# A decoder kernel on one core: the transposes of the heads' probabilities in a new order on TensorE in two of its attention stages

## The chip, the cores and the metric

The kernel runs on one core of a Trainium2 chip. The metric is the device time of one execution in microseconds (us); lower is better. Each engine of the core (TensorE, VectorE, ScalarE, GpSimd) works through its own list of instructions in order, and SyncE issues the DMAs; they meet only at semaphores. In the rows of the profile TensorE is PE (PEld are its weight loads), VectorE is DVE, ScalarE is ACT, GpSimd is POOL.

## The reference, cut to what matters

Two decoder layers over 16 batches of 256 rows with 512 channels. The two stages that the change touches are the cross attention of the first layer (causal) and the cross attention of the second one, which is followed in the same stage by the last linear layer:

```python
x = x + _L0_attn_ref(_layernorm(x), ...)
x = x + _L0_xattn_ref(_layernorm(x), ctx_1024, ctx_1024, ...)      # stage "cross0"
x = x + _L0_ffn_ref(_layernorm(x), ...)
x = x + _L1_attn_ref(_layernorm(x), ...)
x = x + _L1_xattn_ref(_layernorm(x), ctx_1024, ctx_1024, ...)      # stage "last"
x = x + _L1_ffn_ref(_layernorm(x), ...)                            # stage "last"
...
scores = jnp.einsum('bhqd,bhkd->bhqk', Q, K) / jnp.sqrt(jnp.float32(D_K))
...
attn = jax.nn.softmax(scores, axis=-1)
heads = jnp.einsum('bhqk,bhkd->bhqd', attn, V)
```

There are 16 heads of 32 channels, so a head's scores are 256 by 256, in two tiles of 128 rows (T = 2).

## The kernel before, in words

Five stages run one after the other: self attention, cross attention ("cross0"), the experts, a normed attention, and "last". In cross0 and last each batch of 256 rows is one turn of a loop, and the steps of neighbouring batches are interleaved: a step with "-" belongs to the batch before, one with "+" to the batch after. The order of the steps is written out by hand for each engine in the table ORDERS (from line 175), and each engine executes its own list word by word. `over_batches` (line 94) makes 18 turns of it, of which the first and the last ones hold only the steps whose batch exists.

The steps on TensorE:

- X0, X1: four transposes each of the normed rows; Q0 to Q3: projections for four heads each (24 matmuls in cross0, where the keys are made too, 12 in last); V: values (cross0 only); O0, O1: output projection of a half of the rows, 12 matmuls of 512 columns.
- S0 to S3: scores of four heads into four PSUM banks, one bank for each head of a group.
- T0 to T15: the transposes of one head's probabilities (three in cross0, four in last), `prob_transposes`, lines 659 and 2124. All heads use the same single PSUM bank, TP. So T of head h waits until the copy of head h-1 out of the bank is done (`wait_taken`), and until GpSimd has normalised head h (`norm_ok`).
- PV0 to PV3: probabilities times values for four heads, `times_v`, lines 673 and 2137: eight matmuls, for the first 128 keys the four heads, then for the last 128 keys the four heads. Only the latter count up `pv_ok`.
- F0, F1, G0, G1: the last linear layer (last only).

The steps on the other engines: "take h" is the copy of TP into one of eight buffers `probT` (odd heads on ScalarE, even ones on VectorE). It waits for T of its head, and, as the buffer is used again every eight heads, for PV of head h-8:

```python
def take(n, h, off):
    dve.wait_ge(t_full, n * H + h + 1)
    after(dve, pv_ok, n, H, h - NPT + 1, off)
    dve.tensor_copy(probT[:, h % NPT, :], TP[:, :]).then_inc(pt_dve, 1)
```

"z v" takes the result of PV v out of the bank Z, first on ScalarE (after PV v, `heads_hi`), then on VectorE (`heads_lo`), after which PV v+1 may start. "max h" (VectorE), "exp h" (ScalarE), "inv h" (VectorE) and "norm h" (GpSimd) make the softmax of head h from its scores; "mask" stands before "max" in cross0. On ScalarE the order around the changed place of cross0 is `take13- z2- take15- Q2 exp4`.

Of the kernel before, what the change touches and what calls it, by code (L numbers as in the profile page):

```python
# [132 lines left out]
class Uses:  # L133
# [20 lines left out]
    def adds(self, key, n):  # L154
# [4 lines left out]
        while True:  # L159
# [3 lines left out]
            if r > self.n_batch or batch_of(r, self.keys[i][1], self.n_batch) is not None:  # L163
# [27 lines left out]
    },  # L191
    "cross0": {
        "PE": (
                "S0 PV1- T12- Q2 T13- Q3 T14- S1 PV2- T15- T0 PV3- T1 V00 T2 S2 T3 V01 T4 O0- T5 S3 T6 X0+ X1+ T7 PV0 T8 O1- T9 "
                "Q0+ T10 Q1+ T11"),
        "ACT": (
                "take13- z2- take15- Q2 exp4 z3- exp5 take1 Q3 exp6 exp7 take3 exp8 exp9 C0+ exp10 exp11 take5 C1+ X0+ take7 "
# [8 lines left out]
    },  # L206
    "last": {
        "PE": (
                "Q2 T15- S1 PV3- T0 Q3 T1 O0- X0+ T2 S2 X1+ T3 O1- T4 Q0+ T5 S3 T6 Q1+ T7 PV0 T8 T9 PV1 T10 F0- F1- S0+ T11 G0- "
                "T12 G1- T13 PV2 T14"),  # L210
        "ACT": (
                "take13- exp2 z2- exp3 take15- z3- Q2 exp4 exp5 exp6 Q3 take1 exp7 X0+ X1+ take3 exp8 exp9 exp10 exp11 Q0+ "
                "take5 exp12 Q1+ take7 exp13 z0 exp14 take9 exp15 F0- F1- take11 exp0+ z1 exp1+"),
        "DVE": (
# [3 lines left out]
        "POOL": (  # L218
                "rstd+ norm2 norm3 norm4 norm5 norm6 norm7 norm8 norm9 frstd- res norm10 norm11 norm12 norm13 norm14 fbias- "
# [2262 lines left out]
```

## Time and profile before

| | us |
|---|---|
| median of 3 runs | 3359.61 (3356.51 to 3359.7) |
| the profiled execution, its own time | 3358.55 |
| its span, first to last instruction | 3356.8 |
| PE busy | 3053.1 |
| DVE busy | 2104.7 |
| ACT busy | 1418.3 |
| POOL busy | 1315.6 |

The span is 1.75 us shorter than the same execution's own time. A row of the timeline gives start and duration; a matmul is pipelined, so the next step can start before the end that is shown for the one before.

### The profile page before, as it was taken

Reading aid. Unit: us, or ns where it says so; the run is one execution under the profiler, and the core shown is the slowest. Engines: PE = TensorE matmul, PEld = TensorE weight load, DVE = VectorE, ACT = ScalarE, POOL = GpSimd, SP = SyncE. Lnnn points to the kernel's source line nnn. Section 1 sums busy time; section 2 is a strip of 40 time slices with the busy share of each in tenths; the row PEclk is TensorE's granted clock in tenths of the full one; section 3 lists DMA queues with packets and bytes.
Section 4 is the critical chain, followed back from the end, with each engine's and each line's share of the span. In section 5 each row is a group of like instructions: output and inputs, shape, how many; then the busy total and the mean of one; then the engine's idle time right before and its main releaser. Section 6 shows DMA issues by size and latency. Waiting matters only on the chain. (4 is left out here: it accounts for less than half of the span.)

```text
span 3356.8 us, 72149 instructions
## 1 busy us (share of the span) xinstructions
PE 3053.1 (91%) x23800; PEld 2292.0 (68%) x23800; DVE 2104.7 (63%) x5290; ACT 1418.3 (42%) x4627; POOL 1315.6 (39%) x1983
## 2 busy tenths in 40 slices
PE   7999999999998799999988888878879996999997
PEld 6788888888887688778854433333357774777775
DVE  7676666667664888888862222122157776888885
ACT  5344444444443555555551111111122224777774
POOL 3454454455443344444420000000012224888886
PEclk9999999999998999999999999999889997999999
DMA  3000000100000211111269999999831113222221
GB/s 123 32 19 25 31 19 19 37 19 19 25 25 26 89 61 64 50 50 56 79 247 424 431 433 431 431 431 432 371 122 59 58 56 112 75 86 73 87 84 35
DMA packets 108792, 448.74 MB, mean 134 GB/s; under 512 B 11636, under 2 KB 30072, under 8 KB 100280
## 3 DMA queue, kind: packets, MB, share of 16 engines
q1 hardware_dynamic: 102520, 429.56, 32.7%
q10 hardware_dynamic: 6208, 18.35, 1.4%
q8 instruction: 36, 0.59, 0.1%
q14 instruction: 28, 0.23, 0.0%
HBM read 395.45 MB, written 52.43 MB: 133 GB/s over the span
## 5 line engine op out<-in xcount | busy, mean ns | idle before, releaser
L513 POOL TENSOR_TENSOR cross_prob<-cross_prob,cross_rsum 128x128 f32<-128x128 f32 (+1 forms) x512 | 255.3, 528 | 345.7 <-DVE cross_rsum L960 345.4
L513 POOL TENSOR_TENSOR self_prob<-self_prob,self_rsum 128x128 f32<-128x128 f32 (+1 forms) x512 | 287.2, 587 | 245.0 <-DVE self_rsum L960 244.9
L1988 POOL TENSOR_TENSOR last_prob<-last_prob,last_rsum 128x256 f32<-128x256 f32 x512 | 298.3, 612 | 91.9 <-DVE last_rsum L2324 89.6
L766 ACT ACTIVATE self_prob<-self_S,self_neg_max 128x128 f32<-128x128 f32 (+1 forms) x512 | 211.9, 425 | 207.3 <-DVE self_neg_max L952 207.1
L1621 POOL MEMSET norm_minus_half<- 128x2 f32 x1 | 0.1, 99 | 716.6 <-POOLq L52 716.6
L507 POOL TENSOR_TENSOR self_QK_T<-self_QK_T,self_turned 128x512 f32<-128x512 f32 x128 | 166.3, 1299 | 281.1 <-DVE self_QK_T L876 279.3
L2203 ACT ACTIVATE last_prob<-last_S,last_neg_max 128x256 f32<-128x256 f32 x512 | 238.4, 492 | 20.7 <-DVE last_neg_max L2320 20.6
L766 ACT ACTIVATE cross_prob<-cross_S,cross_neg_max 128x128 f32<-128x128 f32 (+1 forms) x512 | 210.2, 429 | 76.8 <-DVE cross_neg_max L952 75.8
L1505 DVE COPY experts_hidT<-experts_T 128x512 f32<-128x512 f32 x32 | 22.1, 692 | 285.0 <-PE experts_T L1394 285.0
L2320 DVE TENSOR_REDUCE last_neg_max<-last_S 128x2 f32<-128x512 f32 x256 | 166.1, 682 | 31.4 <-PE last_S L2114 30.3
L2134 PE MATMUL last_T<-last_ident,last_prob 128*128 128x128 f32 x1024 | 161.8, 281 | 19.1 <-DVE last_probT L2329 15.3
L974 DVE SCALAR_TENSOR_TENSOR self_zTl<-self_Z,self_bv_c,self_zTh 128x256 fp32r<-128x256 f32 x128 | 61.3, 479 | 181.3 <-ACT self_zTh L787 181.3
L2134 PEld LDWEIGHTS last_T<-last_ident,last_prob 128*128 128x128 f32 x1024 | 112.8, 141 | 75.6 <-issue 44.7
L952 DVE TENSOR_REDUCE self_neg_max<-self_S 128x1 f32<-128x128 f32 (+1 forms) x512 | 153.8, 347 | 4.8 <-issue 4.2
L81 PE MATMUL self_A<-self_xTh,self_wqh 128*128 128x256 f32 x512 | 150.8, 294 | 5.2 <-DVE self_xTl L861 5.2
L952 DVE TENSOR_REDUCE cross_neg_max<-cross_S 128x1 f32<-128x128 f32 (+1 forms) x512 | 153.2, 349 | 1.1
L787 ACT ACTIVATE self_zTh<-self_Z,self_bv_c 128x256 fp32r<-128x256 f32 x128 | 60.9, 475 | 211.1 <-PE self_Z L687 211.1
L81 PE MATMUL self_A<-self_xTh,self_wkh 128*128 128x256 f32 x512 | 149.1, 291 | 0.0
L670 PE MATMUL cross_T<-front_ident,cross_prob 128*128 128x128 f32 x768 | 132.8, 282 | 17.7 <-ACT cross_probT L775 11.2
L670 PE MATMUL self_T<-front_ident,self_prob 128*128 128x128 f32 x768 | 131.4, 280 | 18.2 <-POOL self_prob L513 9.3
L83 PE MATMUL self_A<-self_xTh,self_wkl 128*128 128x256 f32 x512 | 145.2, 284 | 0.0
L83 PE MATMUL self_A<-self_xTh,self_wql 128*128 128x256 f32 x512 | 145.0, 283 | 0.0
(332 smaller groups left out, 9713.7 us busy)
## 6 DMA issues: line engine op xcount, KB each, us to landing
late_x<-in_L_ffn_w SPq DMA_DIRECT2D x32, 4096.0 KB, 38.8
moe_w<-in_L_ffn_w SPq DMA_DIRECT2D x31, 4096.0 KB, 38.5
front_spare<-in_ctx SPq DMA_DIRECT2D x32, 512.0 KB, 8.3
front_x_t<-in_x SPq DMA_DIRECT2D x16, 512.0 KB, 3.6
self_res<-in_x SPq DMA_DIRECT2D x16, 512.0 KB, 3.6
x<-self_res SPq DMA_DIRECT2D x16, 512.0 KB, 2.8
front_x_t<-x SPq DMA_DIRECT2D x16, 512.0 KB, 5.4
cross_res<-x SPq DMA_DIRECT2D x16, 512.0 KB, 3.6
```

The costliest lines, as they stand in the source:

```text
L81: pe.matmul(out, ah, bh, start=first, stop=False)
L83: mm = pe.matmul(out, al, bh, start=False, stop=last)
L507: pool.tensor_tensor(to, to, turned.rearrange("p a s -> p (a s)"), ALU.add).then_inc(rot_ok, 1)
L513: ins = pool.tensor_tensor(pr, pr, rsum[:, h, t:t + 1].to_broadcast([P, KQ[t]]), ALU.mult)
L670: mm = pe.transpose(TP[:, o:o + P], prob[:, h % NP, SOFF[t] + k * P:SOFF[t] + (k + 1) * P], ident[:, :])
L766: ins = act.activation(prob[:, h % NP, SOFF[t]:SOFF[t] + KQ[t]], SC[h % G][:, SOFF[t]:SOFF[t] + KQ[t]], ACT.Exp, bias=neg_max[:, h, t:t + ...
L952: ins = dve.tensor_reduce(neg_max[:, h, t:t + 1], SC[h % G][:, SOFF[t]:SOFF[t] + KQ[t]], AX.X, ALU.max, negate=True)
L974: dve.scalar_tensor_tensor(zTs[1][:, v, :], Z[:, 0:S], bv_c[:, v:v + 1], zTs[0][:, v, :], ALU.add, ALU.subtract).then_inc(z_ok, 1)
L1988: ins = pool.tensor_tensor(pr, pr, rsum[:, h, t:t + 1].to_broadcast([P, S]), ALU.mult)
L2134: mm = pe.transpose(TP[:, o:o + P], prob[:, h % NP, t * S + k * P:t * S + (k + 1) * P], ident[:, :])
L2203: ins = act.activation(prob[:, h % NP, t * S:(t + 1) * S], SC[h % G][:, t * S:(t + 1) * S], ACT.Exp, bias=neg_max[:, h, t:t + 1], scale=1. ...
L2320: dve.tensor_reduce(neg_max[:, h, :], SC[h % G][:, :].rearrange("p (t k) -> p t k", t=T), AX.X, ALU.max, negate=True).then_inc(max_ok, 1)
```

## The change

Only words in the orders move. In cross0, on TensorE, T15 of the batch before goes from behind PV2 to ahead of it. In last, T3 to T8 on TensorE each move ahead of the step that stood before them, so that in a full turn no two T are neighbours. The copies take3, take5 and take7 on ScalarE and take4 and take6 on VectorE each move ahead of one step too; take8 stays in its place.

```diff
     "cross0": {
         "PE": (
-                "S0 PV1- T12- Q2 T13- Q3 T14- S1 PV2- T15- T0 PV3- T1 V00 T2 S2 T3 V01 T4 O0- T5 S3 T6 X0+ X1+ T7 PV0 T8 O1- T9 "
+                "S0 PV1- T12- Q2 T13- Q3 T14- S1 T15- PV2- T0 PV3- T1 V00 T2 S2 T3 V01 T4 O0- T5 S3 T6 X0+ X1+ T7 PV0 T8 O1- T9 "
                 "Q0+ T10 Q1+ T11"),
...
     "last": {
         "PE": (
-                "Q2 T15- S1 PV3- T0 Q3 T1 O0- X0+ T2 S2 X1+ T3 O1- T4 Q0+ T5 S3 T6 Q1+ T7 PV0 T8 T9 PV1 T10 F0- F1- S0+ T11 G0- "
+                "Q2 T15- S1 PV3- T0 Q3 T1 O0- X0+ T2 S2 T3 X1+ T4 O1- T5 Q0+ T6 S3 T7 Q1+ T8 PV0 T9 PV1 T10 F0- F1- S0+ T11 G0- "
                 "T12 G1- T13 PV2 T14"),
         "ACT": (
-                "take13- exp2 z2- exp3 take15- z3- Q2 exp4 exp5 exp6 Q3 take1 exp7 X0+ X1+ take3 exp8 exp9 exp10 exp11 Q0+ "
-                "take5 exp12 Q1+ take7 exp13 z0 exp14 take9 exp15 F0- F1- take11 exp0+ z1 exp1+"),
+                "take13- exp2 z2- exp3 take15- z3- Q2 exp4 exp5 exp6 Q3 take1 exp7 X0+ take3 X1+ exp8 exp9 exp10 exp11 "
+                "take5 Q0+ exp12 take7 Q1+ exp13 z0 exp14 take9 exp15 F0- F1- take11 exp0+ z1 exp1+"),
         "DVE": (
...
-                "inv6 X1+ max10 inv7 max11 inv8 inv9 O1- take4 fstats- inv10 max12 take6 max13 max14 inv11 max15 take8 z0 fapply- "
+                "inv6 X1+ max10 inv7 max11 inv8 inv9 take4 O1- fstats- inv10 take6 max12 max13 max14 inv11 max15 take8 z0 fapply- "
                 "inv12 inv13 inv14 take10 max0+ max1+ max2+ take12 z1 inv15 inv0+ G0- G1-"),
```

## Rows read from the trace of the kernel before

**Rows 1.** The page, busy time, share of the span and instructions of each engine.
```profile
PE 3053.1 (91%) x23800; PEld 2292.0 (68%) x23800; DVE 2104.7 (63%) x5290; ACT 1418.3 (42%) x4627; POOL 1315.6 (39%) x1983
```
**Rows 2.** Windows inside cross0, the experts and last: busy time, PEclk the granted clock.
```profile
1150.00:1690.00 540.00, 528.76 (x4718) 431.66 (x4718) 459.71 (x1461) 314.62 (x1209) 238.36 (x475) 1.00 0.18 64
1780.00:2420.00 640.00, 525.90 (x3532) 259.17 (x3534) 132.36 (x248) 75.16 (x92) 0.00 (x0) 0.93 1.01 431
2850.00:3300.00 450.00, 437.58 (x4029) 329.39 (x4030) 377.99 (x961) 344.04 (x1176) 381.88 (x584) 1.00 0.25 79
```
**Rows 3.** TensorE's waits in the window of cross0: total us, times, longest.
```profile
PE cross_T L670 <- ACT cross_probT L775: 9.9, 15, 0.7
```
**Rows 4.** TensorE's waits in the window of last.
```profile
PE last_T L2134 <- DVE last_probT L2329: 11.0, 14, 0.8
```
**Rows 5.** Timeline of TensorE in cross0: PV2-, T15-, T0, PV3- (start, duration).
```profile
1417.84 0.86 PE L687 MATMUL cross_Z<-cross_probT,cross_V 128*32 128x256 f32 x16
1418.63 0.55 PE L670 MATMUL cross_T<-front_ident,cross_prob 128*128 128x128 f32 x3
1419.83 0.55 PE L670 MATMUL cross_T<-front_ident,cross_prob 128*128 128x128 f32 x3 [0.66 <-ACT cross_probT L775]
1420.31 0.86 PE L687 MATMUL cross_Z<-cross_probT,cross_V 128*32 128x256 f32 x16
```
**Rows 6.** Timeline of ScalarE at the same place: z2-, take15-.
```profile
1418.84 0.38 ACT L785 ACTIVATE cross_zTh<-cross_Z 128x256 fp32r<-128x256 f32 x1 [3.26 <-PE cross_Z L687]
1419.29 0.49 ACT L775 ACTIVATE cross_probT<-cross_T 128x384 f32<-128x384 f32 x1
```
**Rows 7.** Timeline of VectorE at the same place: take14-.
```profile
1417.17 0.56 DVE L967 COPY cross_probT<-cross_T 128x384 f32<-128x384 f32 x1 [1.01 <-PE cross_T L670]
```
**Rows 8.** Timeline of TensorE in last: S2, X1+, T3, first of O1-.
```profile
3081.15 1.15 PE L2114 MATMUL last_S<-last_KT,last_QT 32*128 32x256 f32 x16
3082.23 0.66 PE L2063 MATMUL last_A<-last_ident,last_x_t 128*128 128x128 f32 x4
3082.72 0.60 PE L2134 MATMUL last_T<-last_ident,last_prob 128*128 128x128 f32 x4
3083.07 0.48 PE L81 MATMUL last_A<-last_woh,last_zTh 128*128 128x512 f32 x1
```
**Rows 9.** The same turn: S3, T6, first of Q1+; T7, PV0, T8, T9.
```profile
3088.32 1.15 PE L2114 MATMUL last_S<-last_KT,last_QT 32*128 32x256 f32 x16
3089.39 0.66 PE L2134 MATMUL last_T<-last_ident,last_prob 128*128 128x128 f32 x4
3089.81 0.36 PE L81 MATMUL last_A<-last_xTh,last_wqh 128*128 128x256 f32 x1
...
3091.32 0.60 PE L2134 MATMUL last_T<-last_ident,last_prob 128*128 128x128 f32 x4
3091.84 1.07 PE L2149 MATMUL last_Z<-last_probT,last_V 128*32 128x256 f32 x16
3092.85 0.66 PE L2134 MATMUL last_T<-last_ident,last_prob 128*128 128x128 f32 x4
3094.29 0.66 PE L2134 MATMUL last_T<-last_ident,last_prob 128*128 128x128 f32 x4 [0.78 <-DVE last_probT L2329]
```
**Rows 10.** Timeline of ScalarE in that turn: take3; exp12's two passes, take7.
```profile
3083.41 0.59 ACT L2210 ACTIVATE last_probT<-last_T 128x512 f32<-128x512 f32 x1
...
3090.21 0.47 ACT L2203 ACTIVATE last_prob<-last_S,last_neg_max 128x256 f32<-128x256 f32 x1 [1.18 <-DVE last_neg_max L2320]
...
3090.67 0.47 ACT L2203 ACTIVATE last_prob<-last_S,last_neg_max 128x256 f32<-128x256 f32 x1
...
3091.97 0.59 ACT L2210 ACTIVATE last_probT<-last_T 128x512 f32<-128x512 f32 x1
```
**Rows 11.** Timeline of VectorE in that turn: take8.
```profile
3093.54 0.69 DVE L2329 COPY last_probT<-last_T 128x512 f32<-128x512 f32 x1 [0.82 <-PE last_T L2134]
```
**Rows 12.** Timeline of GpSimd in that turn: norm6 to norm9.
```profile
3084.04 4.73 POOL L1988 TENSOR_TENSOR last_prob<-last_prob,last_rsum 128x256 f32<-128x256 f32 x8
```

## The prediction

> **What bounds the kernel now.** I read the page first: PE is busy for 91% of the span and no other engine for more than 63% [rows 1]. That is a mean over five stages, so I took windows inside the two stages that the change touches. In cross0 TensorE is busy for 528.8 of 540 us, in last for 437.6 of 450, both at a granted clock of 1.00 [rows 2]. TensorE sets the pace of both, and it stands still for only 11 and 12 us of these windows. Next I read TensorE's waits there, to see whether that little is one thing. It is: in cross0 one wait of 0.66 us in each of 15 turns, 9.9 us in all, before T0, ended by a copy on ScalarE [rows 3, 5]; in last one of 0.78 us in each of 14 turns, 11.0 us, before T9, ended by take8 on VectorE [rows 4, 9]. Last I read the timeline of one turn around each place, on every engine, because the question for a reordering is always the same: for each T, when does the copy of the head before it end, and what does that copy wait for.
>
> What the reader should see is that a copy needs three things: its own T, its turn in its engine's list, and a free `probT` buffer, which is to say PV of the head eight before. The order on TensorE covers a copy only if the covering step is not itself what the copy waits for.
>
> All other waits of TensorE in a turn come later than these, and are on copies and evictions that TensorE itself sets off. So what one turn loses at either place moves everything behind it, and I count it in full.
>
> **The change, cross0.** T15 moves ahead of PV2. It can start where PV2 starts now, at 1417.84: take14 ends at 1417.73 [rows 5, 7]. PV2 then starts 0.48 later, the distance from a T to the PV behind it (1419.83 to 1420.31) [rows 5].
> Now the chain that releases T0. On ScalarE the list is z2-, take15-. z2 starts 1.00 after PV2 starts, take15 0.45 after z2, and T0 0.54 after take15 (1417.84, 1418.84, 1419.29, 1419.83) [rows 5, 6]. So T0 comes 1.99 after PV2's start whatever T15 does, since take15 stands behind z2 and z2 waits for the end of PV2. T15 is today inside that time: it ends at 1419.18 and costs nothing. Moved ahead, it costs its 0.48, and PV2 covers nothing of its copy: T0 at 1417.84 + 0.48 + 1.99 = 1420.31 in place of 1419.83.
> That is 0.48 x 15 = 7.2 us. In the turn that drains the stage, S1 and T0 have no batch. T14 and T15 are neighbours there, so T15 can't start earlier than now (it waits for take14), and PV3 comes 0.48 + 1.99 = 2.47 after T15's start instead of T15's 0.55, the 0.11 to its copy (1419.18 to 1419.29), 0.49 and 0.05 = 1.20: 1.3 us more. Cross0: 8.5 us slower.
>
> **The change, last, up to S3.** No step is added; what counts is where the copies get no cover. Distances from start to start: S to the next step 1.08, X1 to T 0.49, T to O1 0.35 [rows 8]; S to T 1.07, T to Q 0.42, the Q block to T 1.51, T to PV0 0.52, PV0 to T 1.01 [rows 9].
> Today S2 to the first matmul of O1 is 3083.07 - 3081.15 = 1.92, with X1 and T3 between. Afterwards it is T3, X1, T4. T4 waits for take3, and only X1 stands between: T3 takes 0.66 behind an S (T6 does), its copy starts 0.03 later (T8 ends 3093.51, take8 starts 3093.54), lasts 0.59, and T4 follows 0.06 behind it (3094.23 to 3094.29) [rows 9 to 11]: 1.34. Without a wait it would be about 0.49 + 0.49 = 0.98 (T to X is not in the trace; I take X to T, four transposes each, bounds 0.35 and 0.52). O1 then starts 1.08 + 1.34 + 0.35 = 2.77 after S2: 0.85 later than today, of which 0.36 is a new stall and the rest the T that is now ahead of S3 instead of behind it. T5, T6 and T7 have O1 (twelve matmuls of 512 columns), Q0 (1.51 us) and S3 (1.07) before them, more than the 0.03 + 0.69 + 0.06 that a copy needs beyond its T's end. So S3 is 0.85 later.
>
> **From S3 to T9.** Today that is 3094.29 - 3088.32 = 5.97 [rows 9]. Afterwards the order is S3, T7, Q1, T8, PV0, T9. T8 waits for take7, and on ScalarE take7 now stands close behind S3 with exp12 ahead of it. exp12 needs the scores of S3 and their maximum, and starts 1.89 after S3's start (3090.21); its two passes take 0.46 each (3090.21, 3090.67), so take7 starts 2.81 and ends 3.40 after S3, and T8 starts at 3.46 where its place in the list would allow 1.07 + 0.42 + 1.51 = 3.00: a second new stall, 0.46. Today exp12 hides under Q1.
> PV0 follows at 3.98. Then take8: it needs the buffer of head 0, so it waits for PV0 itself. PV0's counts come from its last four matmuls, which run side by side, so it is as good as the end of PV0: 1.07, and 0.14 to the start of the waiting instruction (PV2's end 1418.70, z2 1418.84 [rows 5, 6]). take8 starts at 5.19, ends at 5.88, T9 at 5.94. PV0 covers nothing of take8; the distance PV0 to T9 is 1.96 where 1.01 would do.
> So S3 to T9 is 0.03 shorter, and the turn is 0.85 - 0.03 = 0.82 us longer. Counted by stalls: 0.36 + 0.46 + 0.95 = 1.77 come, and the one stall that goes is worth 1.44 - 0.49 = 0.95 (T8 to T9, less what one T needs behind another). Behind T9 the order is as before, and z0, the last linear layer's input and F0 follow take8 as today, later by the same time.
> GpSimd isn't in the way: norm6 to norm9 are done at 3084.04 + 4.73 = 3088.77, norm8 a quarter of that stretch earlier, while T8 would run after 3091 [rows 12]. The DMAs of SyncE hang on S, PV and X1 in an unchanged order, and their data is needed a turn later. 16 turns have these steps; the first and last ones lack some neighbours, and I count them as full ones with 1.5 us either way: 0.82 x 16 = 13.1 us.
>
> **Sum.** 8.5 + 13.1 = 21.6. From the profiled execution's own 3358.55 that is 3380.2; the median of the runs shown is 1.1 higher, so I predict 3381.
>
> A row and a rule of the Trainium skill on the clock: it is 1.00 in both windows though each turn has its stall [rows 2]. The page "TensorE: Matmul & The Clock Gate", section "Part 4: PE-mode transpose", says that transposes don't count as a busy PE in the same way, which would speak against stalls placed among transposes. That is the rival on the clock below, and the trace so far speaks against it.
>
> **Rivals.**
> - *The copies do get cover* (faster). If take15 were ready with T15 and take8 with T8, both stalls would go: 0.66 x 15 + 0.95 x 16 = 25 us, 3334. It turns on one point, whether a copy waits for the PV that now stands behind its T. For T15 it does through z2 in ScalarE's list, for T8 through `pv_ok`; were PV0's count for head 0 early in PV0, some of it would come. Against it: the four counts come together at its end. The Trainium skill, "Perfetto Trace Analysis", section "Matmuls", asks that independent groups use other PSUM banks so that the eviction of one overlaps the next; PV0 writes another bank than T8 and by that rule alone the change would gain as this rival says. 3 in 100.
> - *Only cross0 pays.* In last the waits for take3 and take7 may be shorter than my chain (0.36 and 0.46 would have to vanish), and last comes out even: + 8.5, 3368. 6 in 100.
> - *Absorbed.* A wait later in each turn that doesn't hang on the moved steps takes the delay up, and the time stays at 3360. The waits of TensorE show no second one per turn [rows 3, 4]. 4 in 100.
> - *The clock falls.* More stalls in a turn could bring the granted clock of both stages to what the experts' stage has, 0.93 [rows 2]: (528.8 + 437.6) x 0.075 = 73 us on top, 3454; a part of it is likelier than all. 3 in 100.
> - The forecast: 84 in 100.
>
> **Range.** For the forecast alone: cross0 7.2 to 10; last 0.5 to 1.15 a turn, from the bounds of T to X, from a T4 that hardly waits to copies that each start 0.1 later than I take, so 8 to 18.5. That gives 3375 to 3389. With the rivals nearest to it I give 3371 to 3391. A change of 0.2% (6.7 us) is about what a measurement of this kernel can tell from none. Faster 0.03, within 0.04, slower 0.93.
>
> **What would show it.** In cross0 of the changed kernel: PV2 0.48 behind T15, and T0 still 1.99 behind PV2, with about 1.1 us of idle time before it; the turn 0.48 longer. In last: a T3-T4 distance of 1.34, T8 3.46 and T9 5.94 behind S3, and three waits a turn where one was. The clock 1.00 in both. The prediction is wrong if T0 follows PV2 by less than 1.9, if take8 starts before PV0's end, or if take7 goes ahead of exp12's second pass.

## The result, and the profile after

The median of four runs is 3385.5 us (3381.9 to 3388.3) against 3359.1 (3356.5 to 3359.7): a ratio of 1.0079, with a 95% interval from 1.0065 to 1.0093, or 26.4 us more. (The kernel before now has four runs; the three known before the prediction gave 3359.6.) The profiled execution took 3387.97, 2.5 above the median; its span is 3386.2.

The same rows as before, read in the same order. The page: TensorE is busy for 7 us more than in [rows 1], in a span that is 29 us longer, so most of the loss is waiting, not work.

```profile
PE 3060.1 (90%) x23800; PEld 2295.0 (68%) x23800; DVE 2107.7 (62%) x5290; ACT 1414.3 (42%) x4627; POOL 1314.7 (39%) x1983
```

The same windows of cross0 and last as in [rows 2], then TensorE's waits in each (the first row stands for cross0, beside [rows 3]; the other three for last, beside [rows 4]). Columns of the windows: stretch, length, busy time of PE, PEld, DVE, ACT and POOL, granted clock, DMA share, GB/s.

```profile
1150.00:1690.00 540.00, 524.34 (x4673) 427.58 (x4672) 457.12 (x1446) 308.85 (x1194) 236.44 (x472) 1.00 0.18 63
2850.00:3300.00 450.00, 425.81 (x3888) 318.46 (x3889) 368.76 (x930) 330.79 (x1136) 365.79 (x563) 1.00 0.25 78
```

```profile
PE cross_T L670 <- ACT cross_probT L775: 14.6, 15, 1.1
...
PE last_T L2134 <- DVE last_probT L2329: 11.7, 14, 0.9
PE last_T L2134 <- ACT last_probT L2210: 10.2, 27, 0.8
PE last_A L2095 <- DVE last_xb L2309: 1.2, 8, 0.2
```

In cross0 the one wait of each turn is longer, 0.97 in place of 0.66. In last the wait on VectorE's copy is still there, and 27 waits on ScalarE's copies, two a turn, have come beside it. The clock stays at 1.00.

TensorE around the changed place of cross0 (start, duration): T15, PV2, T0, PV3. It answers to [rows 5].

```profile
1418.11 0.55 PE L670 MATMUL cross_T<-front_ident,cross_prob 128*128 128x128 f32 x3
1418.59 0.86 PE L687 MATMUL cross_Z<-cross_probT,cross_V 128*32 128x256 f32 x16
1420.41 0.55 PE L670 MATMUL cross_T<-front_ident,cross_prob 128*128 128x128 f32 x3 [0.96 <-ACT cross_probT L775]
1420.88 0.86 PE L687 MATMUL cross_Z<-cross_probT,cross_V 128*32 128x256 f32 x16
```

ScalarE there: z2-, then take15-, as in [rows 6].

```profile
1419.59 0.38 ACT L785 ACTIVATE cross_zTh<-cross_Z 128x256 fp32r<-128x256 f32 x1 [3.74 <-PE cross_Z L687]
1419.87 0.48 ACT L775 ACTIVATE cross_probT<-cross_T 128x384 f32<-128x384 f32 x1
```

T15 has long been done when ScalarE comes to its copy: ScalarE first waits for PV2, takes z2 out, and only then turns to T15. PV2 covers nothing.

TensorE in a full turn of last: S2, T3, X1, T4, the first matmul of O1; then S3, T7, T8, PV0, T9. It answers to [rows 8] and [rows 9].

```profile
3097.91 1.15 PE L2114 MATMUL last_S<-last_KT,last_QT 32*128 32x256 f32 x16
3098.98 0.65 PE L2134 MATMUL last_T<-last_ident,last_prob 128*128 128x128 f32 x4
3099.47 0.60 PE L2063 MATMUL last_A<-last_ident,last_x_t 128*128 128x128 f32 x4
3100.41 0.63 PE L2134 MATMUL last_T<-last_ident,last_prob 128*128 128x128 f32 x4 [0.34 <-ACT last_probT L2210]
3100.80 0.48 PE L81 MATMUL last_A<-last_woh,last_zTh 128*128 128x512 f32 x1
...
3106.05 1.15 PE L2114 MATMUL last_S<-last_KT,last_QT 32*128 32x256 f32 x16
3107.13 0.66 PE L2134 MATMUL last_T<-last_ident,last_prob 128*128 128x128 f32 x4
...
3109.60 0.63 PE L2134 MATMUL last_T<-last_ident,last_prob 128*128 128x128 f32 x4 [0.38 <-ACT last_probT L2210]
3110.15 1.07 PE L2149 MATMUL last_Z<-last_probT,last_V 128*32 128x256 f32 x16
3112.06 0.66 PE L2134 MATMUL last_T<-last_ident,last_prob 128*128 128x128 f32 x4 [0.83 <-DVE last_probT L2329]
```

ScalarE in that turn: take3; the first pass of exp12, take7. It answers to [rows 10].

```profile
3099.67 0.60 ACT L2210 ACTIVATE last_probT<-last_T 128x512 f32<-128x512 f32 x1 [1.50 <-PE last_T L2134]
...
3107.94 0.47 ACT L2203 ACTIVATE last_prob<-last_S,last_neg_max 128x256 f32<-128x256 f32 x1 [1.66 <-DVE last_neg_max L2320]
...
3108.86 0.60 ACT L2210 ACTIVATE last_probT<-last_T 128x512 f32<-128x512 f32 x1
```

VectorE in that turn: take8, which answers to [rows 11].

```profile
3111.31 0.69 DVE L2329 COPY last_probT<-last_T 128x512 f32<-128x512 f32 x1 [1.55 <-PE last_Z L2149]
```

The reader should look at the releaser in that row. In [rows 11] it was `last_T`, the transpose; now it is `last_Z`, which is PV0. T8 started 1.7 us before, and its copy still can't start, since it writes into the buffer of head 0 that PV0 reads.

From first to last matmul of the stage, cross0 takes 627.7 us in place of 619.6 (+8.1), last 574.0 in place of 549.9 (+24.1). From the start of one PV3 to the next (PV3 closes a batch; the medians over the full turns), a turn of cross0 takes 37.96 in place of 37.62, and one of last 33.27 in place of 32.18. The two stages together lose 32.2 and the span 29.4, because the stages that the change leaves alone took 2.8 less in this execution than in the one before.

The two ends of last cost more than their share in these two executions. Of its 24.1, 14 turns carry 14 x 1.08 = 15.1; the way to the first PV3 carries 3.9, the last interval 3.5, and the stretch behind it 1.6. TensorE in the first turn: T4, then T5.

```profile
2831.79 0.63 PE L2134 MATMUL last_T<-last_ident,last_prob 128*128 128x128 f32 x4 [0.34 <-POOL last_prob L1988]
2834.99 1.09 PE L2134 MATMUL last_T<-last_ident,last_prob 128*128 128x128 f32 x4 [2.57 <-DVE last_probT L2329]
```

VectorE there: the low half of X1, max10, max11, inv8 and inv9, then take4.

```profile
2832.17 0.69 DVE L2277 TENSOR_TENSOR last_xTl<-last_A,last_xTh 128x512 fp32r<-128x512 f32 x1 [0.39 <-ACT last_xTh L2191]
2832.78 0.68 DVE L2320 TENSOR_REDUCE last_neg_max<-last_S 128x2 f32<-128x512 f32 x1
...
2833.45 0.67 DVE L2320 TENSOR_REDUCE last_neg_max<-last_S 128x2 f32<-128x512 f32 x1
2834.03 0.22 DVE L2324 RECIPROCAL last_rsum<-last_sums 128x2 f32<-128x2 f32 x2
2834.17 0.67 DVE L2329 COPY last_probT<-last_T 128x512 f32<-128x512 f32 x1
```

The first turn has no O1 that could stand between T4 and T5. T4 starts at 2831.79, but take4 stands behind inv9 in VectorE's list. VectorE waits 0.39 for ScalarE's half of X1 and from there works without a pause through everything up to take4. In the order before, the Q0 block stood between T4 and T5. Here TensorE waits 2.57 us, and then T5 takes 1.09 in place of some 0.63. Windows of the first turn, of the last interval of last and of the last matmuls of cross0 show why T5 is slow:

```profile
2834.00:2841.00 7.00, 6.01 (x36) 5.35 (x36) 1.70 (x6) 2.85 (x10) 6.68 (x10) 0.52 0.06 23
3342.00:3349.00 7.00, 6.09 (x47) 3.13 (x45) 2.99 (x13) 3.37 (x13) 4.53 (x9) 0.54 0.01 4
1717.20:1720.30 3.10, 3.08 (x8) 2.47 (x9) 2.81 (x6) 0.00 (x0) 3.10 (x1) 0.59 0.34 131
```

The granted clock is 0.52 to 0.59 here, near the lower of its two levels. Whether the change brings that about is a question for the experiments.

### The profile page after: what moved, and what is told of

It is laid out like the page before. It is cut to its first block and busy times, and to the rows that moved or that the text cites. A ratio compares the mean times of both kernels' runs of the same rounds, so it can differ in the third digit from the quotient of the medians.

```text
span 3386.2 us, 72149 instructions
## 1 busy us (share of the span) xinstructions
PE 3060.1 (90%) x23800; PEld 2295.0 (68%) x23800; DVE 2107.7 (62%) x5290; ACT 1414.3 (42%) x4627; POOL 1314.7 (39%) x1983
## 3 DMA queue, kind: packets, MB, share of 16 engines
q1 hardware_dynamic: 102520, 429.56, 32.6%
## 5 line engine op out<-in xcount | busy, mean ns | idle before, releaser
L82 PE MATMUL self_A<-self_xTl,self_wqh 128*128 128x256 f32 x512 | 145.1, 283 | 0.0
```

The source lines that it names most:

```text
L82: pe.matmul(out, ah, bl, start=False, stop=False)
```

## The experiments

Those of each group ran on one chip, with runs of the kernel before among them: median 3358.7 for the first four, 3359.4 for the last three. "Before" and "after" below are the two kernels of the change. Turns are from one S2 or PV3 to the next, and stage times are those of the profiled execution, which in several kernels is not the median one.

**Cross0 alone.** Only the word in cross0 moves, last is as before.

```diff
-  S1 PV2- T15- T0        (TensorE, cross0)
+  S1 T15- PV2- T0
```

> The order of cross0 as changed, that of last as before. My theory (T0 hangs on PV2, then z2, then take15; T15 ahead of PV2 pushes that chain back): T15 to PV2 0.48, PV2 to T0 1.82, no less; each full turn 0.36 longer, the stage 8 us longer, the time 3367. Rival (the stages act on each other through the clock or the data, and cross0 alone is harmless): 3360.

Measured: 3364.0 (3359.7 to 3368.7), ratio 1.0017 [1.0008, 1.0026], so 5.3 us. Cross0 takes 627.7, as in the whole change, with turns of 37.93 and T0 1.82 behind PV2. The turns and T0 are as expected; the time is 3 us short of the expected 3367, while the profiled execution took 3366.9. In that execution last takes 2.6 more than before though its order and its turns are unchanged: its last matmuls ran in a stretch with a granted clock of 0.53.

```profile
3336.00:3343.00 7.00, 5.83 (x21) 4.09 (x14) 0.48 (x1) 0.47 (x1) 0.06 (x1) 0.53 0.21 77
```

So up to 2.6 us at the end of last may come whatever order it has, and are not to be put down to the change. The reverse holds for cross0: in the profile of the run with take7 ahead of exp12 (below), where cross0 has its old order, the first 3.4 us of its last twenty-four matmuls ran at a clock of 0.51 and the stretch behind PV3 took the same 1.6 longer.

**Last alone.** Last as changed, cross0 as before.

> The order of last as changed, that of cross0 as before. My theory: three waits a turn (0.34 before T4, 0.38 before T8, 0.83 before T9), a turn 1.1 longer, plus 9 us in the first turn and the drain, where the clock falls to half: the stage 24 us longer, the time 3380 to 3384. If the steady turns were all of it, 3375. The two single changes add up to the whole (26 us) within 4 us if the stages don't act on each other.

Measured: 3377.2 (3376.1 to 3382.8), 1.0060 [1.0047, 1.0074], so 18.6 us; last takes 574.0 with turns of 33.27, the same as in the whole change. That is between the two expectations, 3375 for the full turns alone and 3380 to 3384 with 9 us at the ends; the profiled execution, 3382.8, is the slowest of the five, so its 24 us for last is more than the usual cost. The parts add up, 5.3 + 18.6 = 23.9 against 26.4, within what these medians can tell: nothing shows that the two edits act on each other.

**Sixteen buffers.** It takes away what take8 waits for. Last as changed, but each head has a `probT` of its own.

```diff
-    NP = NPT = 8
+    NP, NPT = 8, 16
...
-                after(dve, pv_ok, n, H, h - NPT + 1, off)
+                after(dve, pv_ok, n, H, 1 if off < 0 else h - NPT + 1, off)
```

> As e2, but last has 16 buffers for the transposed probabilities in place of 8, so that take8 no longer waits for PV0. My theory (take8 waits for PV0 through the buffer): the wait of 0.83 before T9 goes, T9 follows PV0 by 1.0 instead of 1.9, a turn is 0.8 shorter than in e2, 12 us in all, and the other two waits stay. Rival (take8 is late because VectorE's list is full with the maxima, or since T8 itself is late): T9 stays 1.9 behind PV0 and the time stays that of e2.

Measured: 3380.5 (3374.6 to 3382.7), 1.0063 [1.0048, 1.0078]; last 573.6, turns 33.41. No gain; the expectation of some 12 us was missed. TensorE and VectorE show where it went. TensorE: PV0, T9, the first matmuls of PV1.

```profile
3072.01 1.07 PE L2149 MATMUL last_Z<-last_probT,last_V 128*32 128x256 f32 x16
3073.01 0.66 PE L2134 MATMUL last_T<-last_ident,last_prob 128*128 128x128 f32 x4
3074.36 0.42 PE L2149 MATMUL last_Z<-last_probT,last_V 128*32 128x256 f32 x4 [0.69 <-DVE last_zTl L2333]
```

VectorE: take8, z0.

```profile
3072.21 0.69 DVE L2329 COPY last_probT<-last_T 128x512 f32<-128x512 f32 x1 [0.58 <-PE last_T L2134]
3073.82 0.48 DVE L2333 SCALAR_TENSOR_TENSOR last_zTl<-last_Z,last_bv_c,last_zTh 128x256 fp32r<-128x256 f32 x1 [0.92 <-ACT last_zTh L2216]
```

The mechanism is confirmed: with its own buffer take8 runs beside PV0, and T9 follows PV0 by 1.00, without a wait. But PV1 needs the bank Z that PV0 has filled, and now waits for z0; it starts 2.35 behind PV0, where in the kernel after it was 2.49. Of the 0.83 that went, 0.69 came back at once, one step further on. The turn is even 0.14 longer: T4 waits 0.42 in place of 0.34 and F0 some 0.30 for VectorE where it had waited 0.15 or not at all. I had priced the wait before T9 and not looked at what is late next. This kernel also bears on the clock: it has the same wait before T5 in the first turn, 2.56, yet ran the 9 us behind it, and the last interval too, at a clock of 1.00.

```profile
2830.80:2840.00 9.20, 8.12 (x84) 6.40 (x88) 4.68 (x12) 6.02 (x22) 7.16 (x11) 1.00 0.08 25
3338.00:3351.00 13.00, 9.96 (x96) 5.73 (x96) 7.12 (x21) 7.14 (x21) 11.24 (x17) 1.00 0.01 2
```

**take7 ahead of exp12.** It takes away the wait before T8. Last as changed, one pair exchanged on ScalarE.

```diff
-  take5 Q0+ exp12 take7 Q1+        (ScalarE, last)
+  take5 Q0+ take7 exp12 Q1+
```

> As e2, but on ScalarE take7 stands ahead of exp12. My theory (T8 waits for take7, and take7 for exp12, exp12 for the maximum of S3): the wait of 0.38 before T8 goes, T8 follows S3 by 3.0 to 3.1 instead of 3.55, a turn is 0.4 to 0.5 shorter than in e2, 6 us in all. Rival (the maximum on VectorE or GpSimd's pass is what T8 waits for, not the order on ScalarE): no change from e2, or longer, as exp12 to exp15 come later and S0 of the next batch waits for them.

Measured: 3369.5 (3364.4 to 3371.6), 1.0031 [1.0019, 1.0042]. The turn is 32.66, 0.61 shorter than with last as changed. TensorE's waits in last:

```profile
PE last_T L2134 <- DVE last_probT L2329: 11.7, 14, 0.8
PE last_T L2134 <- ACT last_probT L2210: 4.8, 14, 0.3
```

The 14 waits on ScalarE before T8 are gone (27 became 14), those before T4 and T9 are as they were. So the wait before T8 is caused by exp12 standing ahead of take7, as the prediction says, and it is worth what it shows (0.38) and somewhat more. In the profiled executions last is 14.1 shorter than with last alone: 14 x 0.61 = 8.5, and the rest lies at the ends, whose drain (44.1 against 48.4 from the last S2 on) ran here at a clock of 1.00 up to the wait for the last F0. The medians differ by 7.7, close to the turns' share alone (6 was expected).

**The copy of T15 ahead of z2.** Cross0 as changed, last as before.

```diff
-  take13- z2- take15-        (ScalarE, cross0)
+  take13- take15- z2-
```

> cross0 as changed, and on ScalarE take15 ahead of z2; last as before. My theory (T0 hangs on z2 only through the order on ScalarE): T0 follows PV2 by 0.8 instead of 1.82 and its wait of 0.96 goes. But PV3 waits for z2 on both engines, and from PV2's start that chain is 1.0 + 0.42 + 0.42 and a few hundredths, so PV3 can't come earlier than 1.9 to 2.0 behind PV2 and takes over a wait of about 0.6; a turn comes out 0.1 shorter than before to 0.1 longer, the time 3358 to 3360. If nothing else waited, the turn would be 0.7 shorter than before and the time 3349. Rival (T0 waits for something else, take14 or GpSimd's pass): no change from the changed cross0 alone, 3364.

Measured: 3367.6 (3359.7 to 3370.6), 1.0023 [1.0013, 1.0032]; turns of 37.83. TensorE: PV2, T0, PV3, then T1.

```profile
1419.82 0.86 PE L687 MATMUL cross_Z<-cross_probT,cross_V 128*32 128x256 f32 x16
1420.61 0.55 PE L670 MATMUL cross_T<-front_ident,cross_prob 128*128 128x128 f32 x3
1421.72 0.86 PE L687 MATMUL cross_Z<-cross_probT,cross_V 128*32 128x256 f32 x16 [0.56 <-DVE cross_zTl L972]
1422.83 0.44 PE L670 MATMUL cross_T<-front_ident,cross_prob 128*128 128x128 f32 x2 [0.26 <-DVE cross_probT L967]
```

T0 now starts 0.79 behind PV2 and waits for nothing: it was z2 in ScalarE's list that held it. But PV3 waits for z2 0.56, and T1 0.26 for take0, which VectorE comes to late because its own half of z2 is late. Two waits replace one, 0.82 for 0.97. The turn is 0.13 shorter than with cross0 as changed and still 0.21 longer than before, and the time, 8.2 above the kernel before, shows no gain: the expected 3358 to 3360 was missed. The wait of PV3 had been foreseen, that of T1 had not. It is the buffers' result again: PV3 now follows PV2 by 1.90, which is PV2 and both halves of z2, and no order of the T's would make that shorter (this last is argued, not tried).

**The old order at the ends.** Last as changed, but its first and its last turn have the order of before on TensorE, ScalarE and VectorE.

```diff
+    def steps_of(e, full, r):
+        return EDGE[e] if isinstance(r, int) and r in (0, n_batch - 1) else full
```

> As e2, but the first full turn of last and the turn of the last batch run in the order of before on TensorE, VectorE and ScalarE; all turns between are as changed. My theory (of the 24 us in this stage 9 come from these two turns, with the clock at half in them): the stage 559 + 14 turns of 1.08 = 565 us in place of 574, the clock 1.00 where it was at half in the first turn, the time 3370. Rival (the loss belongs to the full turns, the clock would fall anyway): no change from e2.

Measured: 3372.0 (3371.5 to 3373.7), 1.0045 [1.0030, 1.0061]. Last takes 564.7 with unchanged turns of 33.27, both as expected; the other 9.3 us of last alone's 574.0 were at its ends. By the medians the ends are worth less, 3377.2 - 3372.0 = 5.2. A window of the first turn, of last alone, then of this kernel:

```profile
2826.00:2838.00 12.00, 9.03 (x70) 7.34 (x64) 7.15 (x19) 7.01 (x25) 9.52 (x16) 0.86 0.21 67
```

```profile
2826.00:2838.00 12.00, 10.09 (x100) 7.44 (x100) 6.95 (x20) 10.06 (x38) 10.88 (x18) 1.00 0.21 68
```

The clock is at 1.00 here again, and so it is in the last interval. But that alone doesn't show that the old order keeps it there. Three other kernels with the wait of 2.56 or 2.57 before T5 (sixteen buffers, take7 ahead of exp12, and the last kernel below) were also at 1.00 in the 8 to 9 us behind it, and the drain of the old order ran partly at the lower level in the profiles of cross0 alone and of the copy of T15. So the ends' loss has two parts. With no fall right behind T5 the way to the first PV3 takes 51.9 with take7 ahead of exp12 and 48.9 here, and at a clock of 1.00 the last interval takes 31.2 with sixteen buffers and 30.2 here: about 4 us belong to the order. The other 5 or so are the clock's. This split is an estimate, since it borrows from kernels that differ in one thing more and the first of them has a short fall further on.

**Both copies put right.** The change, with take15 ahead of z2, take7 ahead of exp12 and Q1 on ScalarE behind exp14, and on TensorE PV0 ahead of T8, so that Q1 covers PV0's end and take8.

```diff
-  T7 Q1+ T8 PV0 T9                             (TensorE, last)
+  T7 PV0 T8 Q1+ T9
-  take5 Q0+ exp12 take7 Q1+ exp13 z0 exp14     (ScalarE, last)
+  take5 Q0+ take7 exp12 z0 exp13 exp14 Q1+
```

> cross0 as in e5. In last T3 to T6 stand as changed, but then S3 T7 PV0 T8 Q1 T9 PV1, so that PV0 is done before T8's copy needs its buffer and the Q block covers that copy; on ScalarE take7 ahead of exp12, and z0 exp13 exp14 before Q1. My theory: of the waits of a turn only the 0.34 before T4 stays, PV1 finds z0 done, and a turn takes 31.8 to 32.1 us where before it took 32.19, 2 to 5 us in all; time 3352 to 3358. Rival (ScalarE's exp15, which S0 of the next batch waits for, or VectorE's input of the last linear layer is the next bound): 32.2 to 32.6 a turn, 3358 to 3366.

Measured: 3366.6 (3362.0 to 3370.1), 1.0023 [1.0014, 1.0033]. Cross0 is as in the experiment on the copy of T15, last takes 552.6 with turns of 32.32, 0.14 above before's. TensorE's waits in last:

```profile
PE last_T L2134 <- ACT last_probT L2210: 8.6, 28, 0.3
PE last_A L2095 <- DVE last_xb L2309: 5.3, 14, 0.4
```

The wait before T9, the largest of the kernel before, is gone, and three small ones (before T4, T10 and F0: 0.34, 0.27 and 0.38) add up to more than its 0.78. My theory of 31.8 to 32.1 a turn was missed; the rival put on record with it, that VectorE's input of the last linear layer bounds the turn next, gave 32.2 to 32.6, and that is what came. No kernel here beat the one before.

## Why the prediction was right, point by point

3381 was forecast and 3385.5 measured, inside the range, and the forecast case is the one that came: the chains that it names are in the rows. The closeness of the number is in part luck. By the medians of the single changes cross0 costs 5.3, under its bounds of 7.2 to 10, and last 18.6, at the upper edge of its 8 to 18.5; in the profiled execution last costs 24.1, well outside. Two terms of the sum were mis-sized, in opposite directions. (The upper end of the range, 3389, should by its own terms be 3359.6 + 28.5 = 3388.)

- *T15 in cross0.* PV2 0.48 behind T15, z2 1.00 behind PV2 and T0 0.54 behind take15 came as worked out. T0 follows PV2 by 1.82, not 1.99: take15 starts 0.28 behind z2, not 0.45. By the prediction's own sign (less than 1.9) this piece of it is wrong, though what T0 waits for is right. The step that failed is "T15 is today inside that time ... and costs nothing". In [rows 5, 6] take15 waits for T15's end, 1419.18, so T15 did cost 0.17, and that is given back. The turn grows by 0.34, not 0.48, and its 15 by 5, not 7.2.
- *Cross0's drain.* Forecast 1.3. From T14 to the first matmul behind PV3 it is 1717.22 - 1711.47 = 5.75, where before it was 1712.90 - 1708.46 = 4.44: 1.31. On top came 1.6 that no step of mine holds: the last matmuls ran at a clock of 0.59. Of five profiles with the old order of cross0 one shows the same 1.6, of the four with T15 ahead of PV2 all show the lower level there, so the change may make the fall more likely; it is not its only cause. Cross0: +8.1 for 8.5, two errors that nearly cancel.
- *Last up to S3.* T3 to T4 is 1.43 for 1.34, S2 to O1 2.89 for 2.77, S3 later by 0.97 for 0.85. The chain is the right one; T4 starts 0.14 after the end of take3 (3100.27 to 3100.41) where I had taken 0.06 from take8 and T9.
- *From S3 to T9.* take7 at 2.81 as forecast, T8 at 3.55 for 3.46 (again 0.14 behind its copy), PV0 to T9 1.91 for 1.96, T9 at 6.01 for 5.94. The three waits a turn are 0.34, 0.38 and 0.83. Two of them were then taken away, each by itself: T8's with exp12 out of the way, T9's with a buffer of its own for take8. That T4 waits for take3 rests on the releaser in its row alone.
- *The turn* grew by 1.08, not 0.82. The difference is 0.12 up to S3, 0.07 up to T9, and 0.07 behind T9, where I had assumed none (F0 starts 0.05 later behind the step before it). Over 14 turns 3.6 us.
- *The ends of last* are the largest miss: "I count them as full ones with 1.5 us either way" gives 1.6, and they cost 9 in the profiled execution and 5 by the medians. The experiment with the old order at the ends shows both. The step that failed is that a turn which lacks neighbours costs about what a full one does: where O1 is missing, the reordered lists bring T4 and T5 together while take4 still stands behind VectorE's work up to inv9, one wait of 2.57 us. The clock's part, more than half of the 9 by the estimate above, comes and goes between profiles: the clock fell behind the wait of some 2.57 in two profiles of five. So it can't be put down to the change alone.
- *The rivals.* Covered copies didn't come. That the covering step is what the copy waits for is shown from both sides: T9 with its own buffer and T0 with the copy ahead of z2 do start right behind the PV, without a wait. But the price that I gave this rival, 25 us, was wrong too: PV0 to PV1 and PV2 to PV3 hang on z, and bound the turn just behind. The clock fell in neither steady stage, only at the ends, in stretches of some us. That the full turns, with their transposes and now three stalls, run at a clock of 1.00 speaks, as in the trace before, against the rival for which the prediction names the Trainium skill's page "TensorE: Matmul & The Clock Gate", section "Part 4: PE-mode transpose"; no run here tries transposes alone.

Open: why T4 and T8 start 0.14 behind the end of their copies while T9 and T0 start 0.06 behind (it isn't the copying engine alone, since T4's, T8's and T0's are all ScalarE's); and what decides whether the clock falls at the ends, since the same wait was followed by a fall in some profiles and not in others.

## What to carry to other kernels

Work put between a transpose and the next one hides the copy between them only if the copy waits neither for that work nor for anything in its engine's list that does: for each copy, write down its producer, its buffer's last reader and its neighbour ahead in the list. When a stall goes, take the next wait behind it from the same chain before counting a gain; here the way from one PV to the next through z took back 0.69 of a stall of 0.83 us, and later waits the rest. And read the first and the last turn of a pipelined loop by themselves, since the step that gives cover in a full turn may not exist in them.

## What the runs showed of the hardware

The lower level of the granted clock (0.50; the figure of a window is a mean) came at the ends of the stages and in neither steady window. In the kernel after, behind a wait of 2.57 us in the first turn of last, the granted clock was 0.52 and the transposes took 1.09 in place of 0.63. With the same wait of 2.56 the next 9 us ran at 1.00 in the kernel with sixteen buffers. The last output projection of the same order of last ran at 0.50 in the profile of cross0 alone and at 1.00 in that of the kernel before. A single profile therefore can't tell whether a fall at an end belongs to a change.

VectorE slowed beside GpSimd. In the last kernel the step that turns y into x8 meets GpSimd at work; in the kernel before GpSimd stood idle from 3094.7 to 3096.7, around the same step. VectorE before, its two halves:

```profile
3094.55 0.54 DVE L2302 TENSOR_SCALAR last_x<-last_y,last_mv,last_rstd 128x512 fp8e4<-128x512 f32 x1
...
3095.01 0.54 DVE L2302 TENSOR_SCALAR last_x<-last_y,last_mv,last_rstd 128x512 fp8e4<-128x512 f32 x1
```

VectorE in the last kernel:

```profile
3098.69 1.01 DVE L2302 TENSOR_SCALAR last_x<-last_y,last_mv,last_rstd 128x512 fp8e4<-128x512 f32 x1
...
3099.62 0.83 DVE L2302 TENSOR_SCALAR last_x<-last_y,last_mv,last_rstd 128x512 fp8e4<-128x512 f32 x1
```

GpSimd in the last kernel:

```profile
3097.67 2.50 POOL L1988 TENSOR_TENSOR last_prob<-last_prob,last_rsum 128x256 f32<-128x256 f32 x4
```

The same instruction takes 1.01 and 0.83 us in place of 0.54, and F0's input is later by that, a part of its 0.38 of wait. The Trainium skill, "SBUF — State Buffer", section "Who interferes with whom", says that some forms of tensor_scalar on VectorE share a port pair with GpSimd, and that one blocks the other for a whole instruction. The rows agree with its direction, and so do the 32 instructions of this kind in each of the two profiles. Before, 31 had GpSimd at work for less than a third of their time and took 0.53 to 0.55; the one beside GpSimd took 1.01. In the last kernel 30 had GpSimd beside them and took 0.83 to 1.01, and the other two 0.54. No run here took GpSimd's work away by itself, so this is a strong coincidence and the cause is argued, not shown.
